# A decoder layer in float32: the weights' low parts share storage with the raw weights, in four buffers

## The chip, the cores and the metric

One core of one Trainium2 chip. The metric is the device time in microseconds (us) of one execution, the median of three runs. Smaller is better.

## The reference, cut to what matters

One decoder layer on 2048 tokens (32 sequences of 64) of width 512: linear attention with 32 heads of 128 and a gate, then cross attention, then a product with an identity matrix. The change touches the first of the three:

```python
x = x + _L0_attn_ref(_layernorm(x), qkv_w, out_w, gate_w, norm_w)
# inside, h = 32 heads, d = 128, blocks of 32 tokens
qkv = jax.nn.silu(hidden_states @ qkv_w.T)            # q, k, v per head
scores = einsum('bhnd,bhmd->bhnm', cq, ck) * diag_decay
out = einsum('bhnm,bhmd->bhnd', scores, cv) + inter   # inter: decayed state
xf = attn * rsqrt(mean(attn * attn) + 1e-5)
gate = jax.nn.sigmoid(hidden_states @ gate_w.T)
return gate * (norm_w * xf) @ out_w.T
```

## The kernel before, in words

**Tiling.** The tokens are taken in two halves of 1024, and within a half the heads in eight groups of four (`QUADS`). One pass over one group in one half is called a unit here: 16 units, `body(half, d)` on each engine. `d` from 1 to 6 is a hardware loop, `d` = 0 and 7 (`LAST`) are written out.

**Split numbers.** TensorE multiplies in fp32r. To keep float32's precision each operand is cut in a high part (a copy rounded to fp32r) and a low part (the original less the high part), and each product is three matmuls: high by high, high by low, low by high (L830, L833, L835; L850 to L855 for the values; L887 to L889 for the output).

**Projections.** A unit has eight: values `VA` and `VB`, queries and keys `QK0` to `QK3` of the four heads, gates `G01` and `G23`. Each uses Strassen's scheme in its seven-product form: seven products (`PRODUCTS`) of blocks of the weights by blocks of x. For that the weights' four blocks (512 KB, one DMA) are mixed to seven. The steps for one projection's weights are:

1. SyncE issues the DMA to a raw buffer, in `body` of the sync block (L238).
2. GpSimd mixes, four additions of 128x256 in the raw buffer (`mix`, L329 to L334).
3. ScalarE writes the high parts (`cut`, L418, 1024 and 768 columns) to one of `w_hi_a`, `w_hi_b`, `w_hi_c`.
4. VectorE subtracts and writes the low parts (`cut`, L594) to `w_lo_a`, `w_lo_b` or `w_lo_c`.
5. TensorE runs the 42 matmuls of `project` or the 84 of `project_v`.

There are two raw buffers, `raw0` and `raw1`, and three pairs of `w_hi` and `w_lo`. A raw buffer is refilled when VectorE has written the low part from it: SyncE waits for the count of `w_a`, `w_b` or `w_c`. The output weights (`w_out`, 512 KB, two times a unit, s = 0 and 1) go through `raw1` as well, and become `wo_hi` (ScalarE, L459, which also scales them by `norm_w`) and `wo_lo` (VectorE, L615).

**Seven products and three banks.** The sums of the scheme are built in three PSUM banks, `CHAIN`, `SECOND` and `THIRD`, and intermediate sums are taken out by ScalarE (`snapshot`, L466) while TensorE goes on. TensorE waits in `ready_for` (called in `project`), before products 2, 4, 5 and 6, counted from 0:

```python
if n == 4:
    pe.wait_ge(snapped, count(half, d, 24, 3 * call + 2))
```

On ScalarE the snapshots, the sigmoids and the cuts of later weights are one program in order. For `G01` it is `snapshot` 0 (after product 0), the sigmoid of the first block (L501, after VectorE's first addition, L625), `snapshot` 1 (after product 2), `snapshot` 2 (after product 3), and so on. `cut_out(half, d, 0)` stands ahead of these, `cut_out(half, d, 1)` stands in `G23` between `snapshot` 0 and the first sigmoid (its `first_gap`).

**TensorE's order in a unit.** VA, output tiles 0 and 1 of the previous unit's s = 1, VB, tiles 2 and 3, QK0, tiles 4 and 5, scores, QK1, tiles 6 and 7, scores, G01, the weighing of the values, QK2, output tiles 0 and 1 of s = 0, scores, tiles 2 and 3, QK3, tiles 4 to 7, scores, G23, weighing. In GpSimd's order a mix is followed by `last_block` (L349), the product of one block of a projection with its sigmoid, or by `squares` (L360).

Of the kernel before, what the change touches and what calls it, by code (L numbers as in the profile page):

```python
# [16 lines left out]
F32 = mybir.dt.float32  # L17
# [30 lines left out]
class Prepared:  # L48


    def __init__(self, sb, sem, ctx_in, consts):
        self.ctx_in = ctx_in
        self.consts = consts
        self.raw = [sb(f"raw{i}", [P, 7, 2 * P]) for i in range(2)]
        self.ctx, self.crossed = (r[:, 0:4].rearrange("p (t r) n -> p t (r n)", t=2) for r in self.raw)
# [11 lines left out]
def decoder_layer(nc, x, ctx_in, w_pairs, w_out, norm_w, decay, ident_in, wq_in, wk_in, wv_in, bq_in, bk_in,  # L67
                  bv_in, eye_in, out):
    with ExitStack() as both:
# [3 lines left out]
        def sem(name):  # L73
# [8 lines left out]
        pre = Prepared(lambda name, shape, dt=F32: sb(both, name, shape, dt), sem, ctx_in,  # L82
                       (wq_in, wk_in, wv_in, bq_in, bk_in, bv_in))
# [12 lines left out]
def attention(nc, sb, sem, bank, attn_acc, sq_acc, ident, ones, pre, x, w_pairs, w_out, norm_w, decay, ident_in):  # L96


    with ExitStack() as own:
# [3 lines left out]
        w_lo = [sb(own, f"w_lo_{n}", [P, 7, 2 * P], F32R) for n in "abc"]  # L103
        wo_hi = sb(own, "wo_hi", [P, HG, D], F32R)
        wo_lo = sb(own, "wo_lo", [P, HG, D], F32R)
        raw0, raw1 = pre.raw
# [31 lines left out]
        raw0_landed, raw1_landed = sem("raw0_landed"), sem("raw1_landed")  # L138
        mixed0, mixed1 = sem("mixed0"), sem("mixed1")
# [1358 lines left out]
```

## Time and profile before

| | |
|---|---|
| median of 3 runs | 2142.59 us (2142.46 to 2144.4) |
| the profiled execution, its own time | 2141.13 us |
| its span, first to last instruction | 2139.3 us |
| mean granted TensorE clock | 0.993 of full speed |
| TensorE busy | 2082.8 us, 97% of the span |
| VectorE, ScalarE, GpSimd busy | 1399.9, 1126.9, 759.7 us (65%, 53%, 36%) |
| moved by DMA | 109.49 MB, mean 51 GB/s |

The profiled execution lies 1.8 us above its span and 1.5 us below the median of the runs. Busy shares are over the whole span. "Busy" of TensorE counts pipelined matmuls, so a start-to-start distance says more on its pace than the duration of one.

### The profile page before, as it was taken

The page shows a single profiled execution, that of the slowest core. Times are in us where ns is not written, and L with a number is a line of the kernel's source. Part 1 is how long each engine was busy: PE and PEld are TensorE (multiplying, and loading weights), DVE is VectorE, ACT ScalarE, POOL GpSimd, SP SyncE. Part 2 cuts the span into 40 slices and gives each one's busy share as a digit, 9 for nine tenths or more (in the row PEclk, how much of TensorE's full clock was granted, in tenths as well). Part 3 has the DMA queues.
Part 4 walks back from the last instruction along what each step waited for, and adds up shares of the span by engine and source line. Part 5 has one row for each costly group of instructions (what it writes and reads, how often), then busy time and mean ns, then how long its engine had stood idle before and what let it go on. Part 6 is the DMA issues. An engine that isn't in the chain of part 4 may idle for free. (4 is left out here: it accounts for less than half of the span.)

```text
span 2139.3 us, 42512 instructions
## 1 busy us (share of the span) xinstructions
PE 2082.8 (97%) x16208; PEld 1702.6 (80%) x16208; DVE 1399.9 (65%) x1989; ACT 1126.9 (53%) x1927; POOL 759.7 (36%) x882
## 2 busy tenths in 40 slices
PE   5999999999999999999999999999999999799998
PEld 5788888888888888888888888888888887466665
DVE  6666666665656667766666656666665656588885
ACT  4555455554545455554555545454555544466664
POOL 6343334252525243634343343343342523111110
PEclk9999999999999999999999999999999999799999
DMA  3111211111111111202121111111111111301110
GB/s 128 51 55 42 61 40 59 41 50 50 50 50 51 39 61 31 64 19 61 42 61 41 50 50 41 59 40 60 40 53 48 50 51 35 128 31 47 56 38 20
DMA packets 40502, 109.49 MB, mean 51 GB/s; under 512 B 4960, under 2 KB 9568, under 8 KB 40288
## 3 DMA queue, kind: packets, MB, share of 16 engines
q1 hardware_dynamic: 40128, 107.25, 15.8%
q8 instruction: 59, 0.97, 0.2%
q10 hardware_dynamic: 288, 1.05, 0.1%
q14 instruction: 27, 0.22, 0.0%
HBM read 104.09 MB, written 4.19 MB: 51 GB/s over the span
## 5 line engine op out<-in xcount | busy, mean ns | idle before, releaser
L329 POOL TENSOR_TENSOR raw<-raw 128x256 f32<-128x256 f32 x128 | 129.2, 1009 | 602.4 <-DMA raw<-w_pairs 602.4
L830 PE MATMUL bank<-x_hi,w_hi_c 128*128 128x512 f32 x672 | 267.3, 398 | 2.9 <-DVE v L632 1.5
L835 PE MATMUL bank<-x_hi,w_lo_c 128*128 128x512 f32 x672 | 262.2, 390 | 0.0
L833 PE MATMUL bank<-x_lo,w_hi_c 128*128 128x512 f32 x672 | 261.7, 389 | 0.0
L887 PE MATMUL bank<-wo_hi,y_hi 128*128 128x512 f32 x512 | 205.0, 400 | 4.0 <-DVE y_lo L670 3.0
L888 PE MATMUL bank<-wo_lo,y_hi 128*128 128x512 f32 x512 | 202.7, 396 | 0.0
L889 PE MATMUL bank<-wo_hi,y_lo 128*128 128x512 f32 x512 | 202.7, 396 | 0.0
L360 POOL TENSOR_TENSOR sq_acc<-sq_acc,sq 128x512 f32<-128x512 f32 x124 | 160.5, 1294 | 97.2 <-ACT sq L518 88.0
L632 DVE TENSOR_TENSOR qk<-bank,qk 128x512 f32<-128x512 f32 x192 | 127.3, 689 | 85.2 <-ACT qk L489 42.6
L684 DVE TENSOR_TENSOR attn_acc<-attn_acc,bank 128x512 f32<-128x512 f32 x240 | 163.7, 683 | 21.4 <-PE bank L889 20.0
L830 PE MATMUL bank<-x_hi,w_hi_a 128*128 128x512 f32 x448 | 176.1, 393 | 0.0
L835 PE MATMUL bank<-x_hi,w_lo_a 128*128 128x512 f32 x448 | 175.0, 391 | 0.0
L833 PE MATMUL bank<-x_lo,w_hi_a 128*128 128x512 f32 x448 | 174.7, 390 | 0.0
L466 ACT ACTIVATE qk<-bank 128x512 f32<-128x512 f32 x192 | 115.4, 601 | 109.9 <-PE bank L835 109.1
L830 PEld LDWEIGHTS bank<-x_hi,w_hi_c 128*128 128x128 f32 x672 | 126.0, 188 | 35.3 <-ACT qk L466 5.3
L625 DVE TENSOR_TENSOR gate<-bank,gate 128x512 f32<-128x512 f32 x96 | 66.4, 692 | 124.4 <-PE bank L835 124.4
L835 PEld LDWEIGHTS bank<-x_hi,w_lo_c 128*128 128x128 f32 x672 | 126.1, 188 | 27.2
L833 PEld LDWEIGHTS bank<-x_lo,w_hi_c 128*128 128x128 f32 x672 | 126.2, 188 | 24.7
L349 POOL TENSOR_TENSOR qk<-qk,sq 128x512 f32<-128x512 f32 x64 | 82.6, 1291 | 170.3 <-ACT sq L487 170.3
L625 DVE TENSOR_TENSOR bank<-bank,qk 128x512 f32<-128x512 f32 x128 | 89.5, 699 | 80.5 <-PE bank L835 80.5
L525 ACT ACTIVATE y_hi<-bank 128x512 fp32r<-128x512 f32 x128 | 73.0, 598 | 122.3 <-PE bank L889 111.6
L665 DVE TENSOR_TENSOR bank<-bank,gate 128x512 f32<-128x512 f32 x128 | 82.7, 692 | 80.2 <-ACT sq L518 80.2
(156 smaller groups left out, 5472.1 us busy)
## 6 DMA issues: line engine op xcount, KB each, us to landing
raw<-w_pairs SPq DMA_DIRECT2D x126, 512.0 KB, 3.6
raw<-w_out SPq DMA_DIRECT2D x32, 512.0 KB, 3.6
raw<-ctx_in SPq DMA_DIRECT2D x16, 256.0 KB, 3.1
raw<-ctx_in SPq DMA_DIRECT2D x32, 128.0 KB, 3.1
xr<-x SPq DMA_DIRECT2D x4, 1024.0 KB, 11.5
out<-attn_acc SPq DMA_DIRECT2D x16, 256.0 KB, 2.0
attn_acc<-x SPq DMA_DIRECT2D x8, 256.0 KB, 6.0
decays<-decay SPq DMA_DIRECT2D x32, 64.0 KB, 3.0
```

The lines of the kernel that those rows point to most:

```text
L329: nc.gpsimd.tensor_tensor(raw[:, S1], raw[:, S3], raw[:, A22], ALU.add).then_inc(done, 1)
L360: nc.gpsimd.tensor_tensor(acc, acc, sq[:, b, h], ALU.add).then_inc(sq_added, 1)
L466: nc.scalar.activation(dst, shaped(call, bank[:, (CHAIN, CHAIN, THIRD)[nth]]), ACT.Copy).then_inc(snapped, 1)
L625: nc.vector.tensor_tensor(dst, shaped(call, bank[:, (SECOND, CHAIN, THIRD)[nth]]), src, ALU.add).then_inc(c_added, 1)
L632: nc.vector.tensor_tensor(o, shaped(call, bank[:, at_bank]), o, ALU.mult).then_inc(silu_ready, 1)
L684: nc.vector.tensor_tensor(acc, acc, bank[:, out_bank(i)], ALU.add)\
L830: nc.tensor.matmul(bank[:, to], w_hi[w][:, a, s], x_hi[:, b, c], start=part in ("first", "only") and c == 0, stop=False, skip_group_check= ...
L833: nc.tensor.matmul(bank[:, to], w_hi[w][:, a, s], x_lo[:, b, c], start=False, stop=False, skip_group_check=True)
L835: i = nc.tensor.matmul(bank[:, to], w_lo[w][:, a, s], x_hi[:, b, c], start=False, stop=part in ("last", "only") and c == 1, skip_group_che ...
L887: nc.tensor.matmul(dst, y_hi[:, h, r], wo_hi[:, h], start=(h == 0), stop=False)
L888: nc.tensor.matmul(dst, y_hi[:, h, r], wo_lo[:, h], start=False, stop=False)
L889: k = nc.tensor.matmul(dst, y_lo[:, h, r], wo_hi[:, h], start=False, stop=(h == HG - 1))
```

## The change

- The four tensors `w_lo[k]` and `wo_lo` get the same addresses as four raw buffers `raw[k]` and a fifth, `raw_o`. VectorE's low part of a weight block overwrites the mixed raw block that it is computed from. Projection number `call` (VA 0, VB 1, QK0 2, QK1 3, G01 4, QK2 5, QK3 6, G23 7) uses buffer `call % 4`. The three `w_hi` stay.
- A buffer is refilled when TensorE has finished the projection that used it: SyncE waits for `p_mm` (seven to a projection), and for the output weights for `out_mm`, the count of finished output tiles. The loads stand in another order in SyncE's program. QK0 and QK1 of the first unit are loaded at the start.
- The output weights have a buffer and a semaphore of their own. ScalarE's `cut_out(half, d, 0)` moves from ahead of G01 into it, behind the first sigmoid (`second_gap`).
- The context for the cross attention, which lands in the first two raw buffers, is loaded after the last unit's QK2.

The matmuls, the additions, the copies and their sizes are the same.

```diff
@@ -48,11 +48,15 @@
 class Prepared:
 
 
-    def __init__(self, sb, sem, ctx_in, consts):
+    def __init__(self, sb, same, close, sem, ctx_in, consts):
         self.ctx_in = ctx_in
         self.consts = consts
-        self.raw = [sb(f"raw{i}", [P, 7, 2 * P]) for i in range(2)]
-        self.ctx, self.crossed = (r[:, 0:4].rearrange("p (t r) n -> p t (r n)", t=2) for r in self.raw)
+        self.w_lo = [same(f"w_lo{k}", [P, 7, 2 * P], F32R) for k in range(4)]
+        self.wo_lo = same("wo_lo", [P, HG, D], F32R)
+        close()
+        self.raw = [sb(f"raw{k}", [P, 7, 2 * P]) for k in range(4)]
+        self.raw_o = sb("raw_o", [P, HG, D])
+        self.ctx, self.crossed = (r[:, 0:4].rearrange("p (t r) n -> p t (r n)", t=2) for r in self.raw[:2])
         self.wq = sb("wq2", [P, P])
         self.wk = sb("wk2", [P, P])
...
@@ -234,54 +239,56 @@
 
             @block.sync
             def _(sp):
-                def load(raw, src, landed):
-                    sp.dma_start(raw[:, 0:4], src.rearrange("p (r n) -> p r n", r=4)).then_inc(landed, 16)
+                def load(d, call):
+                    k = call % 4
+                    sp.dma_start(raw[k][:, 0:4], w_pairs[d, call].rearrange("p (r n) -> p r n", r=4))\
+                        .then_inc(raw_landed[k], 16)
+
+                def load_out(d, s):
+                    sp.dma_start(raw_o[:, :, :], w_out[d, s].rearrange("p (h n) -> p h n", h=HG)).then_inc(out_landed, 16)
 
                 sp.dma_start(ident[:, :], ident_in).then_inc(const_landed, 16)
                 for p in range(TT):
                     for t in (p, p + TT):
                         sp.dma_start(attn_acc[:, t], x_t[t]).then_inc(x_tile_landed[t], 16)
+                load(0, QK0)
+                load(0, QK1)
                 sp.dma_start(normw[:, :], norm_w).then_inc(normw_landed, 16)
                 sp.dma_start(decays[:, :, :], decay[:, 0:HG, :]).then_inc(decay_landed, 16)
-                sp.wait_ge(w_b, 2)
-                load(raw0, w_pairs[0, QK0], raw0_landed)
-                sp.wait_ge(w_a, 2)
-                load(raw1, w_pairs[0, QK1], raw1_landed)
 
                 def load_decays(unit):
                     sp.dma_start(decays[:, :, :], decay[:, bass.ds(unit * HG, HG), :]).then_inc(decay_landed, 16)
 
                 def body(half, d):
-                    following = after(half, d)
-                    sp.wait_ge(w_c, count(half, d, 6, 2))
-                    load(raw0, w_pairs[d, G01], raw0_landed)
+                    previous, following = before(half, d), after(half, d)
+                    sp.wait_ge(p_mm, count(half, d, 56, 7 * VB + 7))
+                    load(d, G01)
+                    load(d, QK2)
                     if half == 0 and at(d, 0):
                         sp.dma_start(attn_acc[:, HT:], x_rest[1]).then_inc(x_rest_landed, 16)
-                    sp.wait_ge(w_a, count(half, d, 6, 4))
-                    load(raw1, w_out[d, 0], raw1_landed)
-                    sp.wait_ge(w_b, count(half, d, 4, 4))
-                    load(raw0, w_pairs[d, QK2], raw0_landed)
-                    sp.wait_ge(w_c, count(half, d, 6, 4))
-                    load(raw0, w_pairs[d, G23], raw0_landed)
-                    sp.wait_ge(w_o, count(half, d, 2, 1))
-                    load(raw1, w_pairs[d, QK3], raw1_landed)
+                    sp.wait_ge(p_mm, count(half, d, 56, 7 * QK0 + 7))
+                    load(d, QK3)
+                    sp.wait_ge(p_mm, count(half, d, 56, 7 * QK1 + 7))
+                    load(d, G23)
+                    if previous:
+                        sp.wait_ge(out_mm, count(half, d, 16, 0))
+                    load_out(d, 0)
                     sp.wait_ge(scores_ready, count(half, d, 4, 2))
                     load_decays(2 * d + 1)
-                    sp.wait_ge(w_a, count(half, d, 6, 6))
-                    if not following:
-                        load(raw1, w_out[d, 1], raw1_landed)
-                        return
-                    load(raw1, w_pairs[following[1], VA], raw1_landed)
-                    sp.wait_ge(w_c, count(half, d, 6, 6))
-                    load(raw0, w_pairs[following[1], VB], raw0_landed)
-                    sp.wait_ge(w_a, count(half, d, 6, 8))
-                    load(raw1, w_out[d, 1], raw1_landed)
-                    sp.wait_ge(w_b, count(half, d, 4, 6))
-                    load(raw0, w_pairs[following[1], QK0], raw0_landed)
-                    sp.wait_ge(scores_ready, count(half, d, 4, 4))
-                    load_decays(2 * following[1])
-                    sp.wait_ge(w_o, count(half, d, 2, 2))
-                    load(raw1, w_pairs[following[1], QK1], raw1_landed)
+                    if following:
+                        sp.wait_ge(p_mm, count(half, d, 56, 7 * G01 + 7))
+                        load(following[1], VA)
+                        sp.wait_ge(p_mm, count(half, d, 56, 7 * QK2 + 7))
+                        load(following[1], VB)
...
@@ -291,8 +298,7 @@
                 for dst, src in zip((pre.wq[:, :], pre.wk[:, :], pre.wv[:, :], pre.bias[:, 0:1], pre.bias[:, 1:2],
                                      pre.bias[:, 2:3]), pre.consts):
                     sp.dma_start(dst, src).then_inc(pre.consts_landed, 16)
-                sp.wait_ge(w_c, 2 * QUADS * 6)
-                sp.wait_ge(w_o, 2 * QUADS * 2)
+                sp.wait_ge(p_mm, count(1, LAST, 56, 7 * QK2 + 7))
                 for t in range(2):
                     load_ctx(sp, pre, t)
 
...
-
-                def mix1(half, d, nth, nth_landed):
-
-                    pool.wait_ge(raw1_landed, count(half, d, 80, 16 * nth_landed))
-                    mix(raw1, mixed1, count(half, d, 12, 4 * nth))
+                def mix_pair(half, d, call):
+
+                    k, nth = call % 4, call // 4
+                    pool.wait_ge(raw_landed[k], count(half, d, 32, 16 * nth + 16))
+                    mix(raw[k], mixed[k], count(half, d, 8, 4 * nth))
 
                 def last_block(half, d, call):
                     pool.wait_ge(c_sig, count(half, d, 32, 4 * call + 2))
...
@@ -418,46 +420,43 @@
                     nc.scalar.activation(dst[:, s], raw[:, s], ACT.Copy).then_inc(done, 1)
 
                 def cut_va(half, d, part):
-                    act.wait_ge(mixed1, count(half, d, 12, 4))
-                    cut(w_hi[0], raw1, part, hi_a)
+                    act.wait_ge(mixed[0], count(half, d, 8, 4))
+                    cut(w_hi[0], raw[0], part, hi_a)
 
...
                 def cut_out(half, d, s):
-                    last = s == 1 and half == 1 and at(d, LAST)
-                    act.wait_ge(raw1_landed, count(half, d, 80, 16 * ((3, 6)[s] - last)))
-                    if s or before(half, d):
-                        act.wait_ge(out_mm, count(half, d, 16, 8 * s))
+                    act.wait_ge(out_landed, count(half, d, 32, 16 * s + 16))
                     for h in range(HG):
-                        i = nc.scalar.activation(wo_hi[:, h], raw1[:, 2 * h:2 * h + 2].rearrange("p r n -> p (r n)"),
-                                                 ACT.Copy, scale=normw[:, bass.ds(d * 2 * HG + (s * HG + h), 1)])
+                        i = nc.scalar.activation(wo_hi[:, h], raw_o[:, h], ACT.Copy,
+                                                 scale=normw[:, bass.ds(d * 2 * HG + (s * HG + h), 1)])
                     i.then_inc(hi_o, 1)
...
                 def snapshot(half, d, call, dst, nth):
@@ -494,11 +493,13 @@
                     nc.scalar.activation(result(call, 1, 0), shaped(call, bank[:, CHAIN]),
                                          ACT.Sigmoid).then_inc(c_sig, 1)
 
-                def project_gate(half, d, call, first_gap):
+                def project_gate(half, d, call, first_gap, second_gap=None):
                     snapshot(half, d, call, gate[:, 0, 0], 0)
                     first_gap()
                     act.wait_ge(c_added, count(half, d, 24, 3 * call + 1))
                     nc.scalar.activation(gate[:, 0, 0], gate[:, 0, 0], ACT.Sigmoid).then_inc(c_sig, 1)
+                    if second_gap:
+                        second_gap()
                     snapshot(half, d, call, gate[:, 0, 1], 1)
                     snapshot(half, d, call, gate[:, 1, 1], 2)
                     act.wait_ge(c_added, count(half, d, 24, 3 * call + 2))
@@ -551,8 +552,7 @@
                     project(half, d, QK1)
                     for part in range(2):
                         cut_qk2(half, d, part)
-                    cut_out(half, d, 0)
-                    project_gate(half, d, G01, lambda: None)
+                    project_gate(half, d, G01, lambda: None, lambda: cut_out(half, d, 0))
                     weighted(half, d, 0)
                     project(half, d, QK2, lambda: cut_qk3(half, d, 0), lambda: cut_qk3(half, d, 1))
                     for part in range(2):
...
-                def cut(n, raw, part, done):
+                def cut(n, k, part, done):
                     s = slice(0, 4) if part == 0 else slice(4, 7)
-                    nc.vector.tensor_tensor(w_lo[n][:, s], raw[:, s], w_hi[n][:, s].bitcast(F32),
+                    nc.vector.tensor_tensor(w_lo[k][:, s], raw[k][:, s], w_hi[n][:, s].bitcast(F32),
                                             ALU.subtract).then_inc(done, 1)
 
...
@@ -823,6 +823,7 @@
                         pe.wait_ge(c_added, count(half, d, 24, 3 * call + 2))
 
                 def project(half, d, call, w):
+                    lo = w_lo[call % 4]
                     for n, (a, b, to, part) in enumerate(PRODUCTS):
                         ready_for(half, d, call, n)
                         for c in range(2):
@@ -832,7 +833,7 @@
                                              skip_group_check=True)
                             nc.tensor.matmul(bank[:, to], w_hi[w][:, a, s], x_lo[:, b, c], start=False, stop=False,
                                              skip_group_check=True)
-                            i = nc.tensor.matmul(bank[:, to], w_lo[w][:, a, s], x_hi[:, b, c], start=False,
+                            i = nc.tensor.matmul(bank[:, to], lo[:, a, s], x_hi[:, b, c], start=False,
                                                  stop=part in ("last", "only") and c == 1, skip_group_check=True)
                         i.then_inc(p_mm, 1)
 
```

**ScalarE around G01, in the loop.** The names: `gate<-bank` is a snapshot, `gate<-gate` a sigmoid, `wo_hi<-raw,normw` the output weights' high part. Before:

```order
L418 ACTIVATE w_hi_c<-raw 128x768 [waits mixed0]
L455 ISA
L457 REGISTER_ALU [waits raw1_landed]
L459 ISA [waits out_mm]
L459 ACTIVATE wo_hi<-raw,normw 128x512
L459 ISA
L459 ACTIVATE wo_hi<-raw,normw 128x512
L465 REGISTER_ALU
L466 ACTIVATE gate<-bank 128x512 [waits p_mm]
L500 REGISTER_ALU
L501 ACTIVATE gate<-gate 128x512 [waits c_added]
```

Of the change:

```order
L465 ACTIVATE gate<-bank 128x512 [waits p_mm]
L499 REGISTER_ALU
L500 ACTIVATE gate<-gate 128x512 [waits c_added]
L456 ISA
L458 ISA [waits out_landed]
L458 ACTIVATE wo_hi<-raw_o,normw 128x512
L458 ISA
L458 ACTIVATE wo_hi<-raw_o,normw 128x512
L464 REGISTER_ALU
L465 ACTIVATE gate<-bank 128x512 [waits p_mm]
```

The two instructions on `wo_hi` have moved past the first snapshot and the first sigmoid, and stand directly ahead of the second snapshot.

**SyncE's loads in the loop.** Before, the output weights of s = 0, QK2, G23 and QK3:

```order
L238 ISA [waits w_a]
L238 DMA raw<-w_out 128x1024
L262 ISA
L238 ISA [waits w_b]
L238 DMA raw<-w_pairs 128x1024
L238 ISA [waits w_c]
L238 DMA raw<-w_pairs 128x1024
L266 ISA
L238 ISA [waits w_o]
L238 DMA raw<-w_pairs 128x1024
```

Of the change, QK3, G23 and the output weights of s = 0 (G01 and QK2 stand ahead, behind one wait for `p_mm`):

```order
L244 ISA [waits p_mm]
L244 DMA raw<-w_pairs 128x1024
L271 REGISTER_ALU
L244 ISA [waits p_mm]
L244 DMA raw<-w_pairs 128x1024
L274 REGISTER_ALU
L248 ISA [waits out_mm]
L248 DMA raw_o<-w_out 128x1024
```

The output weights' load has moved from the first of these to the last, and from a wait for VectorE to one for TensorE's last output tile of the previous unit. TensorE's and GpSimd's instructions stand in the order of before, with other waits on GpSimd.

## Rows read from the trace of the kernel before

**Rows 1.** The page, part 1: busy us, share of the span, instructions.

```profile
PE 2082.8 (97%) x16208; PEld 1702.6 (80%) x16208; DVE 1399.9 (65%) x1989; ACT 1126.9 (53%) x1927; POOL 759.7 (36%) x882
```

**Rows 2.** What TensorE waited for: total us, times, longest.

```profile
PE bank L887 <- DVE y_lo L670: 3.0, 3, 2.0
PE bank L865 <- DVE qk L632: 2.9, 2, 1.5
...
PE bank L830 <- ACT qk L466: 1.1, 1, 1.1
```

**Rows 3.** One unit as a stretch: each engine's busy us, clock, DMA share, GB/s.

```profile
580.49:691.29 110.80, 110.80 (x888) 93.86 (x885) 69.98 (x100) 57.51 (x92) 43.33 (x47) 1.00 0.15 49
```

**Rows 4.** Timeline of TensorE at G01: start us, us, line, operands.

```profile
521.19 0.40 PE L889 MATMUL bank<-wo_hi,y_lo 128*128 128x512 f32 x1
...
522.60 0.50 PE L830 MATMUL bank<-x_hi,w_hi_b 128*128 128x512 f32 x1
522.94 0.39 PE L833 MATMUL bank<-x_lo,w_hi_b 128*128 128x512 f32 x1
523.17 0.40 PE L835 MATMUL bank<-x_hi,w_lo_b 128*128 128x512 f32 x1
...
528.18 0.39 PE L830 MATMUL bank<-x_hi,w_hi_b 128*128 128x512 f32 x1
```

**Rows 5.** Timeline of ScalarE over the same G01.

```profile
521.75 1.33 ACT L459 ACTIVATE wo_hi<-raw,normw 128x512 fp32r<-128x512 f32 x2 [0.64 <-PE bank L889]
...
526.47 0.63 ACT L501 ACTIVATE gate<-gate 128x512 f32<-128x512 f32 x1 [1.58 <-DVE gate L625]
527.01 0.60 ACT L466 ACTIVATE gate<-bank 128x512 f32<-128x512 f32 x1
```

**Rows 6.** Line 459 of ScalarE, one instruction of the output weights' high parts: min/median/max.

```profile
L459 ACT ACTIVATE wo_hi<-raw,normw x64: 707/712/724, 78.8 to 1803.1; 128x512 fp32r<-128x512 f32 x64
```

**Rows 7.** Timeline where TensorE resumed upon ScalarE, last unit.

```profile
1769.50 0.63 ACT L466 ACTIVATE qk<-bank 128x512 f32<-128x512 f32 x1
...
1770.18 0.50 PE L830 MATMUL bank<-x_hi,w_hi_c 128*128 128x512 f32 x1 [1.06 <-ACT qk L466]
1770.52 0.39 PE L833 MATMUL bank<-x_lo,w_hi_c 128*128 128x512 f32 x1
```

**Rows 8.** The page, part 6: DMA issues, KB each, us to landing.

```profile
raw<-w_out SPq DMA_DIRECT2D x32, 512.0 KB, 3.6
```

**Rows 9.** Timelines of TensorE and ScalarE at the same place of G23.

```profile
566.62 0.40 PE L889 MATMUL bank<-wo_hi,y_lo 128*128 128x512 f32 x1
...
570.21 1.32 ACT L459 ACTIVATE wo_hi<-raw,normw 128x512 fp32r<-128x512 f32 x2
571.90 0.63 ACT L501 ACTIVATE gate<-gate 128x512 f32<-128x512 f32 x1 [0.36 <-DVE gate L625]
...
573.60 0.39 PE L830 MATMUL bank<-x_hi,w_hi_c 128*128 128x512 f32 x1
```

**Rows 10.** Mixes on GpSimd (min/median/max ns), and timeline of mix and cuts around QK3.

```profile
L329 POOL TENSOR_TENSOR raw<-raw x128: 721/743/1745, 4.8 to 1772.3; 128x256 f32<-128x256 f32 x128
...
547.01 0.95 DVE L594 TENSOR_TENSOR w_lo_a<-raw,w_hi_a 128x768 fp32r<-128x768 f32 x1
...
549.57 1.22 DVE L594 TENSOR_TENSOR w_lo_c<-raw,w_hi_c 128x1024 fp32r<-128x1024 f32 x1
...
551.77 1.09 POOL L329 TENSOR_TENSOR raw<-raw 128x256 f32<-128x256 f32 x1 [6.19 <-DMA raw<-w_pairs]
...
554.74 0.70 DVE L625 TENSOR_TENSOR bank<-bank,qk 128x512 f32<-128x512 f32 x1 [0.69 <-PE bank L835]
...
1772.57 1.57 DVE L594 TENSOR_TENSOR w_lo_a<-raw,w_hi_a 128x1024 fp32r<-128x1024 f32 x1
```

**Rows 11.** ScalarE's second snapshot in QK3, and TensorE's matmul behind it.

```profile
556.01 0.60 ACT L466 ACTIVATE qk<-bank 128x512 f32<-128x512 f32 x1
...
557.18 0.39 PE L830 MATMUL bank<-x_hi,w_hi_a 128*128 128x512 f32 x1
```

More of the change, by code:

```diff
@@ L102, in attention @@
         w_hi = [sb(own, f"w_hi_{n}", [P, 7, 2 * P], F32R) for n in "abc"]
-        w_lo = [sb(own, f"w_lo_{n}", [P, 7, 2 * P], F32R) for n in "abc"]
+        w_lo, wo_lo, raw, raw_o = pre.w_lo, pre.wo_lo, pre.raw, pre.raw_o
         wo_hi = sb(own, "wo_hi", [P, HG, D], F32R)
-        wo_lo = sb(own, "wo_lo", [P, HG, D], F32R)
-        raw0, raw1 = pre.raw
         decays = sb(own, "decays", [P, HG, SEQ])
@@ L282, in body @@
-                    load_decays(2 * following[1])
-                    sp.wait_ge(w_o, count(half, d, 2, 2))
-                    load(raw1, w_pairs[following[1], QK1], raw1_landed)
+                    if following:
[3 more added lines that the diff above has]
+                        load(following[1], VB)
+                        sp.wait_ge(p_mm, count(half, d, 56, 7 * QK3 + 7))
+                        load(following[1], QK0)
@@ L286, in _ @@
+                    sp.wait_ge(out_mm, count(half, d, 16, 8))
+                    load_out(d, 1)
+                    if following:
+                        sp.wait_ge(scores_ready, count(half, d, 4, 4))
+                        load_decays(2 * following[1])
+                        sp.wait_ge(p_mm, count(half, d, 56, 56))
+                        load(following[1], QK1)
                 for half in range(2):
@@ L364, in body @@
                     if half == 0 and at(d, 0):
-                        mix0(half, d, 1)
+                        mix_pair(half, d, QK0)
                         last_block(half, d, VA)
-                        mix1(half, d, 1, 2)
+                        mix_pair(half, d, QK1)
                     else:
-                        mix1(half, d, 1, 2)
+                        mix_pair(half, d, QK1)
                         last_block(half, d, VA)
                     last_block(half, d, VB)
-                    mix0(half, d, 2)
+                    mix_pair(half, d, G01)
                     last_block(half, d, QK0)
-                    mix0(half, d, 3)
+                    mix_pair(half, d, QK2)
                     last_block(half, d, QK1)
@@ L377, in body @@
                         inv_roots(slice(0, HT), 2 * HT, TT + 1)
-                    mix1(half, d, 2, 4)
+                    mix_pair(half, d, QK3)
                     squares(half, d, 0)
-                    mix0(half, d, 4)
+                    mix_pair(half, d, G23)
                     last_block(half, d, QK2)
@@ L428, in cut_qk0 @@
+                    cut(w_hi[1], raw[1], part, hi_b)
                 def cut_qk0(half, d, part):
-                    act.wait_ge(mixed0, count(half, d, 20, 8))
-                    cut(w_hi[2], raw0, part, hi_c)
+                    act.wait_ge(mixed[2], count(half, d, 8, 4))
+                    cut(w_hi[2], raw[2], part, hi_c)
                 def cut_qk1(half, d, part):
-                    act.wait_ge(mixed1, count(half, d, 12, 8))
+                    act.wait_ge(mixed[3], count(half, d, 8, 4))
@@ L443, in cut_qk2 @@
-                    cut(w_hi[2], raw0, part, hi_c)
+                    act.wait_ge(mixed[1], count(half, d, 8, 8))
+                    cut(w_hi[2], raw[1], part, hi_c)
                 def cut_qk3(half, d, part):
-                    act.wait_ge(mixed1, count(half, d, 12, 12))
-                    cut(w_hi[0], raw1, part, hi_a)
+                    act.wait_ge(mixed[2], count(half, d, 8, 8))
+                    cut(w_hi[0], raw[2], part, hi_a)
                 def cut_g23(half, d, part):
-                    act.wait_ge(mixed0, count(half, d, 20, 20))
@@ L733, in body @@
                         statistics(1, (1, TT + 1), HT + 2)
-                    project(half, d, QK0, lambda: cut_a(half, d, 1, 0))
-                    cut_a(half, d, 1, 1)
+                    project(half, d, QK0, lambda: cut_a(half, d, QK1, 0))
+                    cut_a(half, d, QK1, 1)
                     for i in range(2):
@@ L754, in body @@
                     weighted(half, d, 0)
-                    project(half, d, QK2, lambda: cut_a(half, d, 2, 0))
+                    project(half, d, QK2, lambda: cut_a(half, d, QK3, 0))
                     if before_turning:
@@ L793, in _ @@
                 for part in range(2):
-                    cut_a(0, 0, 0, part)
+                    cut_a(0, 0, VA, part)
                 normalise(0, 1)
```

83 lines of the change are left out of this document (41 added, 42 removed).

## Prediction

> **What bounds the kernel now.** I start with the busy shares: TensorE is busy for 2082.8 of 2139.3 us, 97%, and no other engine is above 65% [rows 1]. A share over the span can hide a stage with another limit, so the next view is a stretch of exactly one unit, from VA's first matmul to the next unit's: 110.80 us long, TensorE busy for 110.80 of them, at the full clock, 2.4 GHz [rows 3]. The sixteen units are thus limited by TensorE's own rate of issue: one 512-column matmul starts 0.23 us after the other [rows 4]. The list of what TensorE waited for names no weight: neither a cut nor a DMA of weights is among its releasers, and what stands there in the attention part is small and belongs to the activations: 3.0 us for `y_lo`, 2.9 for the queries, 1.1 for a snapshot [rows 2]. GpSimd does wait for the DMA of raw weights, 6.19 us ahead of one mix [rows 10], but the result comes in time for TensorE all the same. So earlier loads have nothing to win inside a unit, and every wait that the change puts on TensorE is paid in full, since TensorE has no idle time in a unit that could take it up. The question is only whether it adds one.
>
> **The change, part by part.**
>
> *Storage and refills.* The instructions and their sizes are unchanged, so no engine gets work. The refills now wait for TensorE instead of VectorE. With four buffers I follow each load against its use. G01 and QK2 are issued when VB ends, QK3 when QK0 ends, G23 when QK1 ends, next VA when G01 ends, next VB when QK2 ends, next QK0 when QK3 ends, next QK1 when G23 ends. The tightest is G01: one projection (QK0, 42 matmuls by 0.23, 9.7 us) and two output tiles lie between issue and ScalarE's cut, some 12 us, against a landing of 3.6 us [rows 8] (bound above, two transfers at once: twice that, 7.2) and four mixes of 0.74, 3.0 us [rows 10]: 6.6 to 10.2 us. It holds. All others have a projection more. I cost them at nothing: the cover is the projections between, and if it went, GpSimd's mix would be late next, then ScalarE's cut. The context's load moves earlier and was in time. QK0 and QK1 of the first unit come earlier, but GpSimd mixes them behind the token sums, as before: nothing.
>
> *Output weights, s = 1.* SyncE can issue them only when output tile 7 is done: its last matmul ends at 566.62 + 0.40 = 567.02 [rows 9]. With 3.6 us to land [rows 8] and 0.1 to 0.2 for SyncE's reaction (my estimate) they are there at 570.8. Before, ScalarE began on them at 570.21 [rows 9]: 0.6 us late. The cut takes 1.3 us less 0.1 of overlap, ends the path at 572.0, where the sigmoid started at 571.90, and the snapshot behind it ends at 572.0 + 0.5 + 0.6 = 573.1. TensorE needs it at 573.60 [rows 9]. So 0.5 us remain and the cost is nothing; from a landing 0.5 us later on it is paid.
>
> *Output weights, s = 0.* Landing is no trouble here: tile 7 ends at 521.59 [rows 4], the weights are there at 525.3, and ScalarE comes to them at 527.01. The place in ScalarE's order is. Before, the cut ran from 521.75 to 523.08, in a time when ScalarE had nothing else [rows 5]. Now it stands between the first sigmoid and the second snapshot. The sigmoid starts at 526.47 and can't be earlier, as it waits for VectorE's addition; the snapshot followed it directly at 527.01 and ended at 527.61. TensorE passes its wait for that snapshot with product 4, whose first matmul (number 24) starts at 528.18 [rows 4]. The slack is 0.57 us. The two instructions take 0.71 us each [rows 6] and the next starts 0.1 before an end, as the sigmoid and snapshot show (526.47 + 0.63 against 527.01): 0.62 each, 1.24 for both. The snapshot ends at 528.85, and TensorE can go on 0.05 later, as where it resumed upon a snapshot (1769.50 + 0.63 = 1770.13, matmul at 1770.18) [rows 7]. That is 528.90 in place of 528.18, **0.72 us** in each unit. After a resume the second matmul starts 0.34 after the first, not 0.23 [rows 7]: 0.11 more. I take 0.83; the ends for one unit are 0.72 and 0.83, and below them nothing, if the cut overlaps in a way that no row shows.
>
> Behind the late snapshot stands the third, due after product 3 and needed before product 5, 1.36 us later, which moves along with TensorE. VectorE's part (`wo_lo`) now follows the late `wo_hi`: 528.3 to 529.8, and its next addition waits for product 4 and is free by then. Hence no second delay.
>
> **Sum.** 16 units by 0.83 = 13.3 us. On the profiled execution 2141.13 + 13.3 = 2154.4; the median of the runs is 1.5 above that execution, so 2142.59 + 13.3 = **2155.9 us**, 0.6% slower. About 0.2% (4.3 us) is what a measurement of this kernel can tell from no change.
>
> **A rule on ports.** GpSimd's mixes now move to other times. Next VA's mix started at 551.77, after a wait of 6.19 us for its DMA, so GpSimd was free from 545.58 on; the weights are now there before that. It will run from 545.58 on, beside VectorE's cuts at 547.01 and 549.57 [rows 10]. A mix takes 0.74 us mostly and up to 1.75, and a cut that took 1.22 took 1.57 in the last unit, so the two do slow each other. The Trainium skill says in "SBUF — State Buffer", section "Summary: rules for kernel authors", that a VectorE operation with two SBUF inputs beside a GpSimd operation that reads SBUF blocks the second of them until the first is done. By that rule the cuts would come later by whole mixes, and the sum would be that of the second case below, 2164 us; the trace agrees that they meet, by 1.57 against 1.22 us, and shows no cost to TensorE.
>
> **The rivals.**
> 1. *Forecast: the second snapshot of G01 is late*, 0.83 us a unit, 2155.9. For it: the times above lie within one stretch of the trace, and neither end can move. Chance 0.58.
> 2. *GpSimd's mixes hold VectorE back in QK3 too.* Three cuts, each behind up to a mix of 0.74, make 2.2 us. VectorE has 0.69 us of idle time ahead of QK3's first addition [rows 10] and 0.4 ahead of the scores; behind it ScalarE's snapshot ends at 556.61 and TensorE needs it at 557.18 [rows 11], 0.57 more. 2.2 - 1.1 - 0.57 = 0.5 us a unit, 8 us on top: 2164. Against it: one meeting in the trace cost 0.35, and three of those fit in the idle time. Chance 0.17.
> 3. *The landing of s = 1 is late.* From 0.5 us over 3.6 us on, each further us is paid; a landing of 4.6 us costs 0.5 a unit, 8 us: 2164. Against it: the transfer is alone on the queue. Chance 0.07.
> 4. *No stall: the snapshot is in time.* The place is the same second snapshot; it decides at 0.57 us of delay. If the two cuts delay it by less, because ScalarE passes them faster than 0.62 each from a buffer that TensorE has long left, or because TensorE's product 4 is taken up in its queue, the time stays 2142.6. For it: TensorE's ends are modelled. Against it: 1.24 is more than twice 0.57. It is also the case in which the sharing alone works as intended and changes nothing. Chance 0.13.
> 5. *Faster.* Mixes that come early free GpSimd and VectorE where TensorE waited for activations: if the 3.0, 2.9 and 1.1 us [rows 2] all went and nothing stalled, 2142.6 - 7.0 = 2135.6. Against it: those waits stand behind products and normalisation, not behind mixes. Chance 0.05.
>
> **How the numbers follow.** Time: the first case. The range takes in cases 1 to 4, from 2142 to 2166 us; outside lie the fifth and a part of the edges of the second and third. Slower by over 0.2%: cases 1 to 3, 0.82, less 0.02 for a stall below a third of the reckoned one, 0.80. Within 0.2%: case 4 and that rest, 0.15, of which 0.01 goes to faster for a mix of cases 4 and 5, so 0.14 and 0.06.
>
> **What would show it.** In the profile after, ScalarE's `wo_hi` of s = 0 stands behind the first sigmoid of G01, the second snapshot starts near 1.2 us later, TensorE shows a gap before its 25th matmul of G01, released by ScalarE's snapshot, in all sixteen units, and a unit lasts 111.6 us in place of 110.80. Case 2 would show as the same kind of gap in QK3 and longer cuts, case 3 as ScalarE waiting for the DMA of `w_out` in G23 with a gap in TensorE behind it. A unit of 110.8 us would refute me, and so would a wait of TensorE for a weight's cut, which I have excluded.

## The result, and the profile after

The changed kernel takes 2172.22 us (median of 4 runs, 2171.97 to 2172.49) against 2143.23 us before: a ratio of 1.0135, 95% interval 1.0123 to 1.0147. It is slower by 29 us, and above the range of the prediction. In e4 below, one of the four executions took 4128.57 us, nearly twice the other three (2156.54 to 2159.03); its ratio leaves that one out, its median of 2157.9 does not.

First the page of the changed kernel, parts 1 and 5 (instructions as line, engine, operation, operands, count; busy us, mean ns; idle before). It answers to [rows 1] and [rows 10].

```profile
PE 2106.2 (97%) x16208; PEld 1698.9 (78%) x16208; DVE 1421.6 (65%) x1989; ACT 1126.7 (52%) x1927; POOL 859.1 (40%) x882
...
L834 PE MATMUL bank<-x_lo,w_hi_c 128*128 128x512 f32 x672 | 265.9, 396 | 0.0
...
L335 POOL TENSOR_TENSOR raw<-raw 128x256 f32<-128x256 f32 x128 | 128.2, 1001 | 115.7 <-DMA raw<-w_pairs 115.6
```

TensorE has the same 16208 instructions and is busy for 2106.2 us, 23 more. One matmul with the low part of x and `w_hi_c` lasts 396 ns, where the page of before has 389. The idle time of GpSimd ahead of its mixes has fallen to 115.7 us from 602.4: the loads do come earlier, as the change means them to, and the time is longer all the same.

TensorE's list of waits, against [rows 2]:

```profile
PE bank L831 <- ACT gate L465: 7.5, 17, 0.8
PE bank L888 <- DVE y_lo L670: 4.9, 3, 2.3
...
PE bank L866 <- DVE qk L632: 2.9, 2, 1.5
```

There is a new wait on a snapshot of the gate: 16 of the 17 are in G01, one in every unit, and the longest, 0.83 us, is in the first unit's G23. `y_lo` has grown by 1.9 us. The wait in G01, on TensorE's timeline in the unit that answers to [rows 4], and ScalarE's, against [rows 5]:

```profile
536.65 0.40 PE L834 MATMUL bank<-x_lo,w_hi_b 128*128 128x512 f32 x1
536.88 0.40 PE L836 MATMUL bank<-x_hi,w_lo 128*128 128x512 f32 x1
537.72 0.50 PE L831 MATMUL bank<-x_hi,w_hi_b 128*128 128x512 f32 x1 [0.44 <-ACT gate L465]
538.06 0.40 PE L834 MATMUL bank<-x_lo,w_hi_b 128*128 128x512 f32 x1
```

```profile
535.33 0.63 ACT L500 ACTIVATE gate<-gate 128x512 f32<-128x512 f32 x1 [1.62 <-DVE gate L625]
535.86 1.32 ACT L458 ACTIVATE wo_hi<-raw_o,normw 128x512 fp32r<-128x512 f32 x2
537.09 1.06 ACT L465 ACTIVATE gate<-bank 128x512 f32<-128x512 f32 x2
```

The matmul after 536.88 should start at 537.11 and starts at 537.72, then the next comes 0.34 later, 0.11 more than the usual 0.23: 0.61 + 0.11 = 0.72 us. ScalarE runs the sigmoid, the two cuts and only then the snapshot, which begins at 537.09.

In G23 of this unit the output weights land in time, by the slack of [rows 9]:

```profile
580.87 1.34 ACT L458 ACTIVATE wo_hi<-raw_o,normw 128x512 fp32r<-128x512 f32 x2 [0.50 <-DMA raw_o<-w_out]
582.11 0.61 ACT L500 ACTIVATE gate<-gate 128x512 f32<-128x512 f32 x1
582.63 0.57 ACT L465 ACTIVATE gate<-bank 128x512 f32<-128x512 f32 x1
```

ScalarE waits 0.50 us for the DMA and TensorE for nothing. In the first unit they land too late: ScalarE waits 2.01 us for them, and TensorE is held up.

```profile
131.31 1.34 ACT L458 ACTIVATE wo_hi<-raw_o,normw 128x512 fp32r<-128x512 f32 x2 [2.01 <-DMA raw_o<-w_out]
```

```profile
132.47 0.40 PE L836 MATMUL bank<-x_hi,w_lo 128*128 128x512 f32 x1
133.70 0.50 PE L831 MATMUL bank<-x_hi,w_hi_c 128*128 128x512 f32 x1 [0.83 <-ACT gate L465]
```

By the same reckoning this costs 1.23 - 0.23 + 0.11 = 1.1 us, once.

One unit, as in [rows 3], is now 112.45 us long:

```profile
590.77:703.22 112.45, 112.01 (x888) 93.42 (x884) 71.36 (x100) 57.56 (x92) 49.84 (x47) 1.00 0.15 48
```

That is 1.65 us more, and the stall is 0.72 of them. The rest of this unit's loss is found nowhere in a list of waits. It is in the distance from one matmul's start to the next. Here are the first matmuls of QK0 before and after, where nothing waits, and the first of what follows:

```profile
606.28 0.39 PE L830 MATMUL bank<-x_hi,w_hi_c 128*128 128x512 f32 x1
606.50 0.39 PE L833 MATMUL bank<-x_lo,w_hi_c 128*128 128x512 f32 x1
606.73 0.39 PE L835 MATMUL bank<-x_hi,w_lo_c 128*128 128x512 f32 x1
606.96 0.39 PE L830 MATMUL bank<-x_hi,w_hi_c 128*128 128x512 f32 x1
...
615.80 0.40 PE L887 MATMUL bank<-wo_hi,y_hi 128*128 128x512 f32 x1
```

```profile
616.30 0.39 PE L831 MATMUL bank<-x_hi,w_hi_c 128*128 128x512 f32 x1
616.52 0.40 PE L834 MATMUL bank<-x_lo,w_hi_c 128*128 128x512 f32 x1
616.76 0.40 PE L836 MATMUL bank<-x_hi,w_lo 128*128 128x512 f32 x1
616.99 0.39 PE L831 MATMUL bank<-x_hi,w_hi_c 128*128 128x512 f32 x1
...
626.09 0.39 PE L888 MATMUL bank<-wo_hi,y_hi 128*128 128x512 f32 x1
```

42 matmuls take 9.52 us before and 9.79 after, at the same granted clock of 1.00. Taken over all steady matmuls from 100 to 1780 us (distance of a start to the next one on the timeline, distances over 0.30 us left out, for the values over 0.16), the mean distances in ns are as follows. The last column counts the instructions of the whole kernel.

| | before | after | instructions |
|---|---|---|---|
| projections, high by high | 227.8 | 234.8 | 1344 |
| projections, low part of x | 227.2 | 233.9 | 1344 |
| projections, low part of the weights | 228.0 | 231.6 | 1344 |
| values (256 columns), mean of all | 119.9 | 118.2 | 2688 |
| output tiles, mean of all | 232.5 | 230.9 | 1536 |

The timeline rounds starts to 10 ns, which moves the mean of a single kind by up to 1 ns: from the trace's unrounded starts the three kinds after are 233.8, 234.7 and 231.8. The mean over the three is the same either way, 227.7 before and 233.4 after, and only that mean is used below where it matters.

The sum: projections 4032 by 5.77 = 23.2 us, values 2688 by -1.7 = -4.6, output tiles 1536 by -1.6 = -2.5, together 16.1; the stall in G01 16 by 0.72 = 11.5; the one in the first G23 1.1; `y_lo` 1.9. That makes 30.6 of the 31.1 us between the two spans; 0.5 us are not assigned.

### The profile page after: what moved, and what is told of

The parts are those of the page before. It is cut to its first block and busy times, and to the rows that moved or that the text cites. A ratio compares the mean times of both kernels' runs of the same rounds, so it can differ in the third digit from the quotient of the medians.

```text
span 2170.4 us, 42216 instructions
## 1 busy us (share of the span) xinstructions
PE 2106.2 (97%) x16208; PEld 1698.9 (78%) x16208; DVE 1421.6 (65%) x1989; ACT 1126.7 (52%) x1927; POOL 859.1 (40%) x882
## 5 line engine op out<-in xcount | busy, mean ns | idle before, releaser
L836 PE MATMUL bank<-x_hi,w_lo 128*128 128x512 f32 x1344 | 529.4, 394 | 0.0
L836 PEld LDWEIGHTS bank<-x_hi,w_lo 128*128 128x128 f32 x1344 | 252.2, 188 | 61.7
L854 PE MATMUL bank<-w_lo,x_hi 128*128 128x256 f32 x896 | 252.7, 282 | 0.0
L335 POOL TENSOR_TENSOR raw<-raw 128x256 f32<-128x256 f32 x128 | 128.2, 1001 | 115.7 <-DMA raw<-w_pairs 115.6
L854 PEld LDWEIGHTS bank<-w_lo,x_hi 128*128 128x128 f32 x896 | 169.6, 189 | 0.6
L340 POOL TENSOR_TENSOR raw<-raw 128x256 f32<-128x256 f32 x128 | 139.8, 1092 | 0.0
```

The source lines that it names most:

```text
L335: nc.gpsimd.tensor_tensor(raw[:, S1], raw[:, S3], raw[:, A22], ALU.add).then_inc(done, 1)
L340: nc.gpsimd.tensor_tensor(raw[:, S4], raw[:, A12], raw[:, S2], ALU.subtract).then_inc(done, 1)
L836: i = nc.tensor.matmul(bank[:, to], lo[:, a, s], x_hi[:, b, c], start=False, stop=part in ("last", "only") and c == 1, skip_group_check=True)
L854: nc.tensor.matmul(dst, x_hi[:, b, c, s], w_lo[c][:, a], start=False, stop=False, skip_group_check=True)
```

## The experiments

The distances of starts in this part are means as in the table above, each from the timeline of the run.

All runs are set against runs of the kernel before on the same chip; the ratios have their 95% intervals. Differences from the changed kernel's 2172.22 us, or between two runs of different parts, are less sure: the medians of the kernel before that go with them lie between 2142.9 and 2143.99.

**1. The place of the cut in ScalarE's order.** Two runs: the changed kernel with the cut one place earlier, and the kernel before with the cut moved as the change moves it.

```diff
-                    project_gate(half, d, G01, lambda: None, lambda: cut_out(half, d, 0))
+                    project_gate(half, d, G01, lambda: cut_out(half, d, 0))
```

> The changed kernel with ScalarE's cut of the output weights (s = 0) moved forward by one place in G01, ahead of the first sigmoid, as it already stands in G23. Theory A (a late second snapshot stalls TensorE): the gap of 0.84 us before the 25th matmul of G01 goes, 0.72 us a unit, 11.6 us in all: 2160.6 from 2172.2. The pace of the projections' matmuls, 233 ns from start to start, stays. Rival (the gap is only where a stall shows that lies elsewhere, with the projections' slower pace): it comes back at another matmul and the time stays within 2 us of 2172.

Measured: 2160.12 us, ratio 1.0078 (1.0061 to 1.0095), 12.1 below the changed kernel. In G01 ScalarE now waits 0.68 us for the DMA and is through in time:

```profile
530.61 1.34 ACT L458 ACTIVATE wo_hi<-raw_o,normw 128x512 fp32r<-128x512 f32 x2 [0.68 <-DMA raw_o<-w_out]
531.85 0.61 ACT L500 ACTIVATE gate<-gate 128x512 f32<-128x512 f32 x1
532.38 0.57 ACT L465 ACTIVATE gate<-bank 128x512 f32<-128x512 f32 x1
```

The 25th matmul starts 5.71 us after the first of its projection (527.63 and 533.34); in the changed kernel it was 6.31 (531.41 and 537.72). The projections' pace stayed at 233.4 ns.

```diff
-                    cut_out(half, d, 0)
-                    project_gate(half, d, G01, lambda: None)
+                    project_gate(half, d, G01, lambda: None, lambda: cut_out(half, d, 0))
```

> The kernel before, with nothing but ScalarE's cut of the output weights (s = 0) moved behind the first sigmoid of G01. Theory A: 0.72 us a unit, 11.6 us slower, 2155, at an unchanged pace of 227 ns. Rival (the move costs only together with the late landing of the output weights): no gap, 2143.

Measured: 2156.28 us, ratio 1.0062 (1.0045 to 1.0079), 12.3 above the kernel before, at 227.8 ns. Its list of waits has the wait and no other new one:

```profile
PE bank L831 <- ACT gate L466: 8.0, 16, 0.5
```

So theory A holds from both sides: the move alone costs 12 us with either storage, and the late landing has no part in it.

**2. Alignment to 64 bytes.** The two kernels differ in where tensors lie. In the changed one the low parts start at an odd multiple of 32 bytes. I tested that by spacers.

```diff
+        sb(both, "spacer0", [P, 8])
         with ExitStack() as early:
...
         self.raw_o = sb("raw_o", [P, HG, D])
+        sb("spacer1", [P, 8])
```

> The changed kernel with two spacers of 32 bytes a partition, so that the low parts start at a multiple of 64 bytes as they did in the kernel before (in the changed one they start at an odd multiple of 32), and everything behind is moved by 64. Theory B (alignment of the low parts sets the pace): 233 ns falls to 227, 4032 matmuls by 6 ns, 24 us: about 2149. Rival C (the distance or the region of the addresses, or the in-place use, sets it): pace and time stay, 2172.

Measured: 2162.88 us, ratio 1.0091 (1.0074 to 1.0108): 9.3 below the changed kernel, not 24.

```diff
+        sb(own, "spacer0", [P, 8])
         w_lo = [sb(own, f"w_lo_{n}", [P, 7, 2 * P], F32R) for n in "abc"]
+        sb(own, "spacer1", [P, 8])
```

> The kernel before, with the three low-part tensors alone shifted by 32 bytes. Theory B (alignment): the projections' matmuls go from 227 to about 233 ns, 24 us slower, 2167. Rival C: unchanged, 2143.

Measured: 2157.9 us, ratio 1.0062 (1.0041 to 1.0082). The projections' mean distance went to 233.4 ns, as theory B has it, but the time rose by 13 to 14 us and not by 24; the values got faster by 1.9 ns (the table at the end of this part), which is 5 of the 10 us missing. The other way round the distance only fell to 231.8. Both expectations of theory B fit in sign and neither in size: the start of the low parts matters, its alignment to 64 does not explain it. Rival C had spoken of region or in-place use; e4 changes neither and is slower, so at least a part is neither.

**3. Larger alignments.** In the kernel before x's parts, the high parts and the low parts all start 256 bytes past a multiple of 1024. The next runs put the changed kernel's tensors there (spacers of 608 and 416 bytes), or only at multiples of 128 (96 and 32 bytes), with the first repair too, and shift the kernel before by 64 bytes as a whole.

> The changed kernel with spacers of 608 and 416 bytes, so that x's parts, the high parts and the low parts all start at 256 bytes past a multiple of 1024, as in the kernel before. Theory B' (the start within 1024 bytes sets the pace): the projections' matmuls go back to 227.7 ns in each of the three kinds, and the time is before's plus G01's stall, 2155 to 2156. Rival C' (the region of the addresses, or the low parts lying in the buffers that GpSimd and the DMAs also write): the pace stays at 231 to 232 ns, as with the 64-byte alignment, 2163.

Measured: 2157.73 us, ratio 1.0069 (1.0052 to 1.0085); the pace is 227.9 ns. QK0 of a unit takes 9.52 us again (611.92 to 621.44):

```profile
611.92 0.39 PE L834 MATMUL bank<-x_hi,w_hi_c 128*128 128x512 f32 x1
612.14 0.39 PE L837 MATMUL bank<-x_lo,w_hi_c 128*128 128x512 f32 x1
612.37 0.39 PE L839 MATMUL bank<-x_hi,w_lo 128*128 128x512 f32 x1
612.60 0.39 PE L834 MATMUL bank<-x_hi,w_hi_c 128*128 128x512 f32 x1
...
621.44 0.40 PE L891 MATMUL bank<-wo_hi,y_hi 128*128 128x512 f32 x1
```

> The changed kernel with spacers of 96 and 32 bytes: all of those tensors start at a multiple of 128, but no longer at one place within 1024 (768 for the low parts, 384 for the rest). If 128 bytes are what counts, the same as with the places within 1024: 227.7 ns, 2155 to 2156. If more than 128 counts, 230 ns or over, 2160 or over. Rival C': 2163.

Measured: 2163.15 us, ratio 1.0087 (1.007 to 1.0104), 231.8 ns. Multiples of 128 are not enough.

> Both repairs of the changed kernel together: the spacers of the first run and the cut ahead of the first sigmoid. Theories A and B': 2143 to 2144, the kernel before. Rival C': 2151.

Measured: 2144.46 us, ratio 1.0009 (1.0 to 1.0019). Both repairs together bring the kernel before back to within 2 us. So the low parts in the buffers that the DMAs and GpSimd write, the refills that wait for TensorE and the mixes at other times cost little or nothing together. What may be left fits two waits that the trace shows there too: 4.9 us for `y_lo`, 1.9 more than before, and 0.29 us in the first unit's G23.

```diff
+        sb(both, "spacer0", [P, 16])
         pre = Prepared(lambda name, shape, dt=F32: sb(both, name, shape, dt), sem, ctx_in,
```

> The kernel before with everything behind the raw buffers' start moved by 64 bytes (odd multiples of 64 instead of multiples of 128). If 128 bytes count (theory B'), the projections' matmuls go from 227.7 to about 231.8 ns as in the 64-byte aligned version, 16 us less what the values gain: about 2152. If only 64 counts, 2143.5.

Measured: 2143.94 us, ratio 1.0000 (0.999 to 1.001), with 227.8 ns. A common shift of all operands by 64 bytes costs nothing, which points away from where each starts, and to where they start relative to each other.

**4. The distance.** A matmul has two operands: the stationary one, which TensorE's weight load takes, here a block of the weights, and the moving one, here 512 columns of x. Seen by the distance between their starts, the earlier runs fall in line. The start of the low parts less that of x's, within 512 bytes, is 0 in the kernel before and in e5, e7, e8; 416 in the changed kernel; 384 in e2 and e6; 32 in e4. The last runs test the distance in the kernel before itself, by one spacer of 96 or 128 float32 ahead of the low parts, or of 96 ahead of the high parts:

```diff
+        sb(own, "spacer0", [P, 96])
         w_lo = [sb(own, f"w_lo_{n}", [P, 7, 2 * P], F32R) for n in "abc"]
```

> The kernel before with the low parts (and all behind them) 384 bytes further, so that they start at 640 within 1024 and x and the high parts at 256: the distance of the 64-byte and 128-byte aligned versions of the changed kernel. Theory B'': the projections show those versions' pattern, 229, 233.7 and 232.5 ns, the values 117.5 to 119: 12 us less the values' gain of about 5, some 2151 to 2153. Rival C' (region, or buffers that others write, which would leave the distance without effect): 2143.5, unchanged pace.

Measured: 2152.84 us, ratio 1.0046 (1.0031 to 1.0062), with 228.9 ns for high by high, 233.6 for the low part of the weights and 232.5 for the low part of x: the pattern of e2 and e6 to 0.3 ns, in another region and without in-place use.

```profile
609.81 0.39 PE L831 MATMUL bank<-x_hi,w_hi_c 128*128 128x512 f32 x1
610.04 0.39 PE L834 MATMUL bank<-x_lo,w_hi_c 128*128 128x512 f32 x1
610.27 0.40 PE L836 MATMUL bank<-x_hi,w_lo_c 128*128 128x512 f32 x1
610.51 0.39 PE L831 MATMUL bank<-x_hi,w_hi_c 128*128 128x512 f32 x1
...
619.52 0.40 PE L888 MATMUL bank<-wo_hi,y_hi 128*128 128x512 f32 x1
```

> The same with 512 bytes. If the pattern repeats every 512 bytes (the stationary block's 512 bytes a partition), the pace is that of the kernel before, 227.7 and 119.9 ns, 2143.5. If it repeats only at 1024 or more, the pace differs, to either side, by over 2 us.

Measured: 2142.62 us, ratio 1.0000 (0.9991 to 1.0009), 227.6 ns. At 512 bytes it is as at none.

> The kernel before with the high and the low parts 384 bytes further than x, so both differ from x and not from each other. If the distance of the low parts to the high ones counts, unchanged: 2143.5. If the distance of the weights to x counts, all three kinds of the projections' matmuls are slower, by at least what the low parts' shift alone costs: 2151 or more.

Measured: 2160.39 us, ratio 1.0078 (1.0062 to 1.0093), all three kinds slow, 233.3, 232.6 and 232.5 ns in the same order. The distance between the weights and x counts. Where the low parts start by themselves does not explain the slow pace of e6, which has them 768 bytes past a multiple of 1024, as e11 has (256 + 512), which is fast. What the runs do not separate is the step from 231.8 ns at 384 bytes to 233.4 at 32 and 416: in both of the latter the low parts also start at an odd multiple of 32 bytes, and no run shifts all operands together by 32.

**5. A version to beat both.** The output tiles were faster in the versions where `wo_lo` stood 384 bytes off `wo_hi`, so that tensor alone was moved, with both repairs:

```diff
+        same("spacer2", [P, 96])
         self.wo_lo = same("wo_lo", [P, HG, D], F32R)
...
+        sb("spacer3", [P, 96])
         self.raw_o = sb("raw_o", [P, HG, D])
```

> The changed kernel with both repairs and, besides, the output weights' low part alone 384 bytes further within 1024 bytes than their high part. Theory B'' (what counts is where the stationary and the moving operands start relative to each other within some hundred bytes, not where each starts): the output tiles' matmuls go from 232.7 to about 229.6 ns as in the two versions with that distance, the projections stay at 227.7; 1536 by 3.1 ns, 4.8 us below the version with both repairs: 2139.7. Rival C'': no effect of this tensor alone, 2144.5.

Measured: 2142.55 us over 11 runs, ratio 0.9995 (0.9986 to 1.0004). The output tiles went to 230.6 ns on the mean, the projections stayed at 227.7, as theory B'' says; of the 4.8 us that I expected 1536 by 1.9 = 2.9 remain, and the interval does not tell it from the kernel before. It is not shown that it beats either. The distance is also not all that counts for the output tiles: e2 and e6 have the same one between `wo_lo` and `wo_hi`, and ran them at 229.6 ns, 1.0 less.

One thing I overlooked. In the output tiles `y_hi` and `y_lo` are the stationary operands and `wo_hi` and `wo_lo` the moving ones, and by the sizes of the tensors between them `y_hi` starts 128 bytes past `wo_hi`, modulo 512, in every version. Their 232.5 ns are near the projections' pace off 0, not the 227.7 at 0. Whether placing `y_hi` and `y_lo` at 0 would bring them there too was not tried; 1536 by 4.8 ns would be 7 us, by my estimate from these two paces.

All versions side by side (mean distances in ns, each the mean over its three kinds of matmul):

| version | distance of low parts to x, bytes | projections | values | output tiles | us |
|---|---|---|---|---|---|
| before | 0 | 227.7 | 119.9 | 232.5 | 2143 |
| changed | 416 | 233.4 | 118.2 | 230.9 | 2172.2 |
| e1 changed, cut earlier | 416 | 233.4 | 118.1 | 230.9 | 2160.1 |
| e2 changed, 64-byte | 384 | 231.8 | 117.9 | 229.6 | 2162.9 |
| e3 before, cut moved | 0 | 227.8 | 119.9 | 232.5 | 2156.3 |
| e4 before, low parts 32 off | 32 | 233.4 | 118.0 | 232.2 | 2157.9 |
| e5 changed, as before in 1024 | 0 | 227.9 | 119.9 | 232.5 | 2157.7 |
| e6 changed, 128-byte | 384 | 231.8 | 117.9 | 229.6 | 2163.2 |
| e7 is e5 and e1 | 0 | 227.8 | 119.9 | 232.5 | 2144.5 |
| e8 before, all by 64 | 0 | 227.8 | 119.9 | 232.6 | 2143.9 |
| e9 is e7, `wo_lo` off by 384 | 0 | 227.7 | 119.9 | 230.6 | 2142.6 |
| e10 before, low parts by 384 | 384 | 231.7 | 117.8 | 233.0 | 2152.8 |
| e11 before, low parts by 512 | 0 | 227.6 | 119.9 | 232.6 | 2142.6 |
| e12 before, both parts by 384 | 384 (high too) | 232.8 | 118.7 | 232.9 | 2160.4 |

## Why the prediction was wrong

The direction was right, its one term was right, and one was missing.

- **The stall in G01** was forecast at 0.83 us a unit, 13.3 in all, and cost 12.1 and 12.3 us by the two runs of the first experiment. The step on ScalarE's place in its order held as written: slack 0.57 us, two cuts of 0.62. In the kernel before with the cut moved, the 25th matmul comes 6.26 us after the first (526.49 and 532.75) in place of 5.58 [rows 4]: 0.68, and 0.11 for the resume. In the changed kernel it is 0.61 and 0.11; the 24 matmuls ahead of the wait take 5.71 us there without a stall (e1), not 5.58, so TensorE comes to it later.
- **The term that failed** is the first: "the instructions and their sizes are unchanged, so no engine gets work". Unchanged instructions did not mean unchanged time. The addresses of TensorE's operands changed, and with them the distance of starts, from 227.7 to 233.4 ns in the projections: 16.1 us in the sum over all kinds; by the runs with and without the spacers it is 14.5 (changed less e5) and 15.7 (e1 less e7). My reading of [rows 3] and [rows 4], that TensorE's own rate of issue bounds the unit, was right, and its consequence was missed: where that rate is the bound, everything that it depends on is a term, the layout of the operands too. No case of mine had it, which is why the range ended at 2166.
- **The refills** cost nothing, as said: no wait of TensorE for a weight's cut, and e7 equals the kernel before within 2 us.
- **The landing of s = 1** (third case) took 0.50 us of ScalarE's time and none of TensorE's in the unit shown, by the slack forecast. In the first unit the landing took 5.3 us in place of the 3.6 that I had read, which is the median of [rows 8], and the case came true once, for 1.1 us. Why it took longer there is open.
- **GpSimd beside VectorE** (second case): the mixes moved to where I put them, and the two do block each other.

```profile
556.93 1.48 DVE L595 TENSOR_TENSOR w_lo<-raw,w_hi_a 128x768 fp32r<-128x768 f32 x1
557.55 1.45 POOL L340 TENSOR_TENSOR raw<-raw 128x256 f32<-128x256 f32 x1
...
559.53 1.25 DVE L595 TENSOR_TENSOR w_lo<-raw,w_hi_c 128x1024 fp32r<-128x1024 f32 x1
559.78 1.60 POOL L337 TENSOR_TENSOR raw<-raw 128x256 f32<-128x256 f32 x1
...
561.30 0.95 DVE L595 TENSOR_TENSOR w_lo<-raw,w_hi_c 128x768 fp32r<-128x768 f32 x1
561.34 1.50 POOL L338 TENSOR_TENSOR raw<-raw 128x256 f32<-128x256 f32 x1
```

  Mixes of 0.74 us take 1.45 to 1.60 beside VectorE's cuts, a cut that took 0.95 us [rows 10] took 1.48 once, and GpSimd's busy time rose from 759.7 to 859.1 us. By the Trainium skill's "SBUF — State Buffer", section "Summary: rules for kernel authors", the second of the two is blocked; the trace agrees: the mix that issues at 559.78, behind a cut, lasts until 561.38, 0.60 us after that cut's end. Here it was mostly GpSimd that waited, whose lateness reached no matmul. VectorE's busy time rose by 22 us. In QK3 there is no gap: the case was wrong in who pays.
- **The y_lo term** of 1.9 us in the last unit was not forecast. ScalarE sat idle for 2 us ahead of a square with no releaser in the trace (1840.89, "1.99 <-issue"). What it waited for is open.

## What to carry to other kernels

When TensorE issues back to back, look for costs of a change in its matmul start-to-start distance as well as in its waits: compare the distance of a few steady matmuls before and after, at the same granted clock. A change of storage moves every tensor behind it; bring the starts of the moving and the stationary operands back to the distance that they had, modulo 512 bytes, by spacers, before judging the change itself. For the 512-column matmuls in fp32r the distance 0 was the fastest tried, for the 256-column ones it was the slowest. And ahead of a snapshot that TensorE waits for, an engine's order has only the slack that the trace shows (0.57 us here), so a moved instruction is to be set against that, not against the engine's idle share.

## What the runs showed of the hardware

- The distance between 512-column matmuls in fp32r depends on where the stationary operand starts relative to the moving one: 227.7 ns at 0 bytes (and at 512), 231.7 to 231.8 with the low parts 384 bytes off, 233.4 with them 32 or 416 off, 232.8 with the high and the low parts 384 off. A common shift by 64 bytes changes nothing. For the projections only these distances were tried.
- The 256-column matmuls of the values, in which weights and x have changed roles, go the other way: 119.9 ns at 0, 117.8 to 118.2 with the low parts off it and 118.7 with both parts.
- The Trainium skill's "TensorE: Matmul & The Clock Gate", section "Wait — 56ns, not 53.3ns?", gives the columns' time and about 2.5 ns, 215.7 ns at 512 columns. No version here reached that: the best had 227.6 ns, at a granted clock of 1.00. The matmuls here are in fp32r with a new weight load for each, and no run tells which of the two, if either, makes the difference.
- What in the chip makes the difference was not tried: the runs show that the relative start counts, and that it is within the reads of TensorE's two operands is only a reading. Nor is it all: between versions with the same distances the output tiles differ by up to 1.0 ns.
